# A nine-stage token tower: the filter spectrum computed in pieces inside earlier stages, expert weights gathered by GpSimd, and the token stage as one sequence

## What is computed

```python
h = _L0_tok_ref(x, L0_tok_emb, L0_tok_W, L0_tok_b)
h = h + _L0_attn_ref(_layernorm(h, axis=-1), ...)
...
h = h + _L3_attn_ref(_layernorm(h, axis=-1), L3_attn_h0, L3_attn_numerators, L3_attn_denumerator)
h = h + _L3_ffn_ref(_layernorm(h, axis=-1), ...)
```

```python
H_trunc = jnp.fft.rfft(b, n=Lx, axis=-1) / jnp.fft.rfft(a, n=Lx, axis=-1)
h_trunc = jnp.fft.irfft(H_trunc, n=Lx, axis=-1)
H = jnp.fft.rfft(h_trunc, n=2 * Lx, axis=-1)
H_tf = h0.astype(H_causal.dtype) + H_causal
Y = jnp.einsum('bli,ijl->blj', X, H_tf)
```

## Time and profile before

| | |
|---|---|
| median of 3 runs | 849.91 us (846.54 to 850.06) |
| the profiled execution's own time | 854.18 us |
| its span | 852.4 us |
| mean granted clock of TensorE, as a share of full speed | 0.822 |

### The profile page before, as it was taken

How to read it: one execution, slowest core, us unless ns; L and a number is a source line. 1 busy time by engine, 2 the same in 40 slices (tenths; PEclk the granted TensorE clock), 3 DMA queues, 4 the chain that set the end, 5 groups by cost and what they waited for, 6 DMA issues and landing times. The chain is left out here.

```text
span 852.4 us, 12948 instructions
## 1 busy us (share of the span) xinstructions
PE 630.7 (74%) x4476; PEld 418.0 (49%) x4476; DVE 519.1 (61%) x1402; ACT 331.4 (39%) x635; POOL 273.4 (32%) x233
## 2 busy tenths in 40 slices
PE   1489755774879378999759999777877652988774
PEld 1446644653767252322347878672322111984653
DVE  0105588653465747567657884428365898744797
ACT  1123201342545223544335553113432974831453
POOL 6431921414030101001157774322001698600420
PEclk9879768686999558989859996566898866999987
DMA  8652231100000010000000000040000000000011
GB/s 275 192 174 69 76 80 45 66 2 1 1 1 0 1 67 1 0 2 1 33 6 12 13 7 12 1 176 0 1 0 31 5 0 0 2 3 1 1 26 25
DMA packets 18781, 30.02 MB, mean 35 GB/s; under 512 B 6434, under 2 KB 15650, under 8 KB 18082
## 3 DMA queue, kind: packets, MB, share of 16 engines
q1 hardware_dynamic: 16162, 19.80, 7.6%
q0 software_dynamic: 2560, 9.44, 3.5%
HBM read 27.25 MB, written 1.05 MB: 33 GB/s over the span
## 5 line engine op out<-in xcount | busy, mean ns | idle before, releaser
L156 POOL TENSOR_TENSOR norm_rstd<-norm_var,minus_half 128x16 f32<-128x16 f32 x16 | 47.4, 2961 | 316.6 <-DVE norm_var L150 316.6
L1247 ACT ACTIVATE m_g<-PS,w_slot 128x512 f32<-128x512 f32 x96 | 60.7, 685 | 73.4 <-PE PS L1301 64.4
L1200 DVE TENSOR_TENSOR m_gw<-m_g,PS 128x512 f32<-128x512 f32 x96 | 61.3, 682 | 41.1 <-PE PS L1309 27.4
L1301 PE MATMUL PS<-m_xT,w_slot 64*128 64x512 f32 x192 | 70.2, 684 | 6.9 <-ACT m_g L1247 6.8
L1325 PE MATMUL PS<-m_gw,w_slot 128*64 128x512 f32 x192 | 57.2, 666 | 0.0
L252 PE MATMUL PS<-w_base,tok_windows 128*128 128x128 f32 x128 | 21.4, 342 | 29.1 <-DMA tok_windows<-in_emb,tok_ids 21.1
L232 POOL DMA_INDIRECT tok_windows<-in_emb,tok_ids x32 | 30.5, 953 | 22.1 <-PE PS L263 9.6
L1309 PE MATMUL PS<-m_gT,m_sel 48*128 48x512 bf16 x96 | 24.1, 418 | 17.8 <-DVE m_gw L1200 12.1
L2047 ACT COPY rat_xf<-PS 64x512 f32<-64x512 f32 x32 | 33.1, 1034 | 10.4 <-PE PS L2103 10.1
L138 DVE BATCH_NORM_STATS2 norm_halves<-H 128x6 f32<-128x64 f32 x256 | 33.8, 209 | 1.3 <-PEq L2637 1.2
L252 PEld LDWEIGHTS PS<-w_base,tok_windows 128*128 128x128 f32 x128 | 19.4, 180 | 30.7 <-issue 13.3
(11 more groups left out here) (341 smaller groups left out, 1669.0 us busy)
## 6 DMA issues: line engine op xcount, KB each, us to landing
rff_routed<-in_routed SPq DMA_DIRECT2D x64, 129.0 KB, 2.1
rat_hf<-in_rat_taps SPq DMA_DIRECT2D x1, 2048.0 KB, 8.2
w_slot<-in_w_rat SPq DMA_DIRECT2D x1, 1589.0 KB, 12.0
w_slot<-in_w_win SPq DMA_DIRECT2D x1, 1378.5 KB, 5.8
...
```

The lines of the kernel that those rows point to most:

```text
L156: nc.gpsimd.tensor_tensor(N.rstd[:], N.var[:], C.minus_half[:], ALU.pow).then_inc(S["norm_rstd"], 1)
L1200: nc.vector.tensor_tensor(gw[:, i % 2, half, :], g[:, i % 2, half, :], gate_bank[half], ALU.mult)\
L1247: nc.scalar.activation(g[:, i % 2, half, :], hid_bank[(n - 1) % 3], ACT.Gelu, bias=b1[:, s:s + 1])\
L1301: nc.tensor.matmul(hid_bank[n % 3], w1[lane(half), s, :], pair_of(xT, pair)[lane(half)], start=True, stop=True).then_inc(S["hid_ps"], 1)
```

## The change

**Filter.** A class `Filter` takes the place of `Coefficients`. Its taps and constants are loaded in the batch-norm stage. PE transforms steps 0 to 3 in that stage's tail and 4 to 7 at the head of m1. ACT copies both parts out (`move`) and squares the denominator (`square`: steps 0 and 1 in the batch-norm stage, 2 to 7 behind the gelus of m1's steps i = 2 to 7). POOL makes sums and products in m1 (`ratio`, five instructions a step: steps 0 to 2 ahead of `norm_rstd(1)`, 3 to 7 behind it). DVE takes 32 reciprocals of 128 x 128, one in each of m1's steps 16 to 31 and m2's steps 0 to 15. POOL multiplies by them in m2 (`scale`). The rational stage starts with a finished spectrum.

**Rational stage.** The token norms and transforms come first, three of the eight moves to `rat_xf` go from ACT to DVE, four forward transforms and the moves that follow stand among the responses, and three PSUM banks instead of four serve the responses.

**Token and linear stages.** The token stage goes chunk by chunk (`ladder`, spacing 22) instead of in two rounds of four, and takes in the block that loaded the first constants. Expert segments of chunks 0 to 3 are gathered by 32 indirect transfers that POOL issues, 16 behind the window gathers and 16 at the start of the linear stage; SP loads chunks 4 and 5 once the windows of chunk 5 have come, and 6 and 7 in the linear stage. `add_shared` has chunks 0 and 1 ahead of `norm_rstd(1)` and 2, 3 and 4 behind it.

**Transposes that nobody reads.** m1's 24 are gone, m2's 44 stay, and the window stage gets 16 and then 126 in its first part and 70 in its last.

The core of the diff:

```diff
+            C.load(sp, "base")
             C.experts.load_route(sp)
+            sp.wait_ge(gathered[1], 16 * G4)
             C.load(sp, "early")
             C.load(sp, "gate")
-            C.experts.load(sp, range(CHUNKS // 2))
+            sp.wait_ge(gathered[5], 16 * G4)
+            C.experts.load(sp, (4, 5))
...
+            C.experts.gather(pool, range(0, CHUNKS // 4))
+            pool.wait_ge(S["const"], 1)
...
+            ladder([(34, lambda c: turn_windows(c, 0)), (52, lambda c: turn_windows(c, 1)), (71, turn_tails),
+                    (82, convolve), (117, turn_y)], 22)
...
+            C.experts.gather(pool, range(CHUNKS // 4, CHUNKS // 2))
             pool.wait_ge(C.sem("early"), C.count("early"))
-            for c in range(CHUNKS // 2):
+            for c in range(2):
                 C.experts.add_shared(pool, nc.gpsimd.tensor_tensor, c)
                 C.experts.add_bias(nc, C, c)
             norm_rstd(nc, pool, S, C, N, 1)
-            for c in range(CHUNKS // 2, CHUNKS // 2 + 1):
+            for c in range(2, CHUNKS // 2 + 1):
...
+    def find_rows(self, v, C):
+
+        v.wait_ge(self.route_loaded, 16)
+        self.nc.vector.tensor_scalar(self.rows[:], self.route[:, 0:CHUNKS // 2 * SEGS], float(P), C["lane"], ALU.mult, ALU.add)\
+            .then_inc(self.rows_ready, 1)
+
+    def gather(self, pool, chunks):
+
+        pool.wait_ge(self.rows_ready, 1)
+        for c in chunks:
+            for j in range(SEGS):
+                at = c * SEGS + j
+                self.nc.gpsimd.indirect_dma_start(
+                    self.routed[:, c, j, :], None, self.dram["routed"],
+                    bass.IndirectOffsetOnAxis(ap=self.rows[:, at:at + 1], axis=0)).then_inc(self.loaded[c], 16)
...
+        y_banks = [PS[0][:, 1, 0:CW], PS[1][:, 0, 0:CW], PS[1][:, 1, 0:CW]]
+
+        @block.sync
+        def _(sp):
+            C.load(sp, "coef")
+            C.filter.load(sp)
...
+            def move_spectra(s):
+                for k in range(2):
+                    C.filter.move(act, s, k, [PS[2 + k][:]])
+
+            move_spectra(0)
+            move_spectra(1)
...
+            C.filter.square(act, 0)
+            move_spectra(2)
+            C.filter.square(act, 1)
+            move_spectra(3)
...
+                    for s in range(STEPS // 2, 3 * STEPS // 4) if it else range(STEPS // 2):
+                        C.filter.scale(pool, s)
+                else:
+                    for s in range(3, STEPS) if it else range(3):
+                        C.filter.ratio(pool, s, scratch[:])
...
+                    C.filter.invert(v, 2 * STEPS + i)
+                elif i >= n_round:
+                    C.filter.invert(v, i - n_round)
...
+                if again and i < 2:
+                    move_spectra(6 + i)
+                elif again and 2 <= i < 8:
+                    C.filter.square(act, i)
...
-            rouse(nc, C, y_bank[1], 24 if again else 44)
+            if not again:
+                rouse(nc, C, y_bank[1], 44)
...
+                spectra(4)
             for k in range(2):
                 turn_x(0, k)
+            if again:
+                spectra(5)
             logits(0)
             hidden(0)
             hidden(1)
+            if again:
+                spectra(6)
+            pe.wait_ge(S["identb"], 1)
             turn_parts(0)
+            if again:
+                spectra(7)
+                for k in range(2):
+                    pe.wait_ge(C.filter.moved[k], STEPS)
...
+                    rouse(nc, C, PS[3][:, 1, :], 16)
+                if n == 560:
+                    pe.wait_ge(S["h_new"], W + 1)
+                if n % 4 == 0:
+                    if 58 <= n < 228:
+                        rouse(nc, C, PS[3][:, 1, :], 5 if n < 115 else 3 if n < 172 else 1)
+                    if 560 <= n < 660:
+                        rouse(nc, C, PS[0][:, 1, :], 2 if n < 620 else 4)
...
+    def transform(self, pe, C, s, k, to):
+
+        if s == 0 and k == 0:
+            pe.wait_ge(C.sem("coef"), C.count("coef"))
+            pe.wait_ge(self.loaded, 16)
+        if s:
+            pe.wait_ge(self.moved[k], s)
+        for c in range(2):
+            rows = slice((2 * k + c) * QUAD, (2 * k + c + 1) * QUAD)
+            self.nc.tensor.matmul(to[c], C["rat_spectrum"][rows, :], self.taps[rows, s * STEP:(s + 1) * STEP],
+                                  start=True, stop=True).then_inc(self.made[k], 1)
+
+    def move(self, act, s, k, parts):
+        act.wait_ge(self.made[k], 2 * s + 2)
+        raw = self.raw[s][:, k]
+        n = 2 // len(parts)
+        for j, ps in enumerate(parts):
+            ins = self.nc.scalar.copy(raw[:, j * n:(j + 1) * n], ps)
+        ins.then_inc(self.moved[k], 1)
+
+    def square(self, act, s):
+        act.wait_ge(self.moved[1], s + 1)
+        self.nc.scalar.activation(self.of(s), self.raw[s][:, 1], ACT.Square).then_inc(self.squared, 1)
+
+    def ratio(self, pool, s, scratch):
+
+        pool.wait_ge(self.moved[0], s + 1)
+        pool.wait_ge(self.squared, s + 1)
+        of = self.of(s)
+        self.nc.gpsimd.tensor_tensor(self.inv[:, s], of[:, 0], of[:, 1], ALU.add).then_inc(self.power, 1)
+        num, den = self.raw[s][:, 0], self.raw[s][:, 1]
+        if s:
+            pool.wait_ge(self.sums, 2 * s)
+        self.nc.gpsimd.tensor_tensor(scratch, bcast(num[:, 1], 1, 2), den, ALU.mult).then_inc(self.terms, 1)
+        pool.wait_ge(self.terms, 2 * s + 1)
+        self.nc.gpsimd.tensor_tensor(den, bcast(num[:, 0], 1, 2), den, ALU.mult).then_inc(self.terms, 1)
+        pool.wait_ge(self.power, s + 1)
+        pool.wait_ge(self.terms, 2 * s + 2)
+        self.nc.gpsimd.tensor_tensor(of[:, 0], den[:, 0], scratch[:, 1], ALU.add).then_inc(self.sums, 1)
+        self.nc.gpsimd.tensor_tensor(of[:, 1], scratch[:, 0], den[:, 1], ALU.subtract).then_inc(self.sums, 1)
+
+    def invert(self, v, n):
+
+        s, k = n // 4, n % 4
+        at = self.inv[:, s, k * P:(k + 1) * P]
+        v.wait_ge(self.power, s + 1)
+        self.nc.vector.reciprocal(at, at).then_inc(self.inverted, 1)
+
+    def scale(self, pool, s):
+        pool.wait_ge(self.inverted, 4 * s + 4)
+        pool.wait_ge(self.sums, 2 * s + 2)
+        self.nc.gpsimd.tensor_tensor(self.of(s), self.of(s), bcast(self.inv[:, s], 1, 2), ALU.mult).then_inc(self.ready, 1)
...
-            for s in range(STEPS + 1):
-                if s < STEPS:
-                    square(s)
-                if s == 1:
-                    norm_rstd(nc, pool, S, C, N, 1)
-                if s:
-                    ratio(s - 1)
...
+            move_xf(0)
+            move_xf(2)
+            for g in range(PAIRS // 2):
+                if g in (2, 5, 6):
+                    move_xf({2: 4, 5: 6, 6: 7}[g])
+                real_parts(g)
...
+            pe.wait_ge(C.filter.ready, STEPS)
+            for g in range(PAIRS // 2):
+                respond(g)
+                if g in (1, 3, 4, 5):
+                    forward({1: 4, 3: 5, 4: 6, 5: 7}[g])
```

433 lines of the change are left out of this document (211 added, 222 removed).

## The result

The changed kernel takes 898.71 us (median; 897.86 to 899.55) against 849.98 us before: a ratio of 1.058, with an interval of 1.055 to 1.061. The forecast was 838 us. The profiled execution has a span of 897.5 us.

What follows compares the result with a forecast made beforehand. No engine was taken to bound the kernel: stages run one after the other with barriers. Terms -36 + 27 + 10 - 11 - 6 + 3 + 1 = -12 gave 842 us profiled, 838 us median; range 811 to 868.

Steps and rivals of the forecast that it cites:

- the slower rival: Linear stage and m1: POOL's reads hold DVE everywhere, +18 and +37, sum +9, median 859 us; chance 0.28.
- Rational stage, -36: Rational stage: the spectrum's eight steps leave it, so the last response's successor on PE comes 36 us earlier; bounds 30 to 40.
- Token stage, -11: Token stage: 48 gathers instead of 32 bound it; -15, or -4 if DVE's stall returns in full; milder half taken, -11.
- Linear stage, +10: Linear stage: gathers and additions delay POOL's norm, +5.4, plus one more hold of DVE, 4.2 us; bounds +5 to +18.
- m1, +27: First expert stage: four parts, for head, round 1's norm, DVE against POOL, and reciprocals; +27 us, between +11 and +37.
- Part (b): First expert stage: round 1's norm waits behind three ratios, the third waiting for ACT's square; +13 us, between +7 and +16.
- Part (c): First expert stage: DVE against POOL in the second gating and the norm; +3 us, between 0 and +7.
- (a): Head of the first expert stage: 24 transposes go, sixteen matmuls and ACT copies come; +7 us, between +3 and +9.
- (d): First expert stage: sixteen small reciprocals in steps where DVE had room; +4 us, between +1 and +5.
- m2, +1: Second expert stage: sixteen small reciprocals, with POOL's eight products beside steps in which it idles; +1 us, -2 to +4.
- Window stage, -6: Window stage: new transposes raise the clock in the tail, giving 7 us back and costing one; bounds -11 to +5.
- The rival that they do nothing: Window stage and m1: transposes fail to raise the clock, window +3, m1 +30, sum 0, median 850 us; chance 0.12.

Runs made afterwards that it cites:

- e8: The changed kernel, but SP loads all 64 expert segments and POOL gathers none, token stage still one sequence: ratio 1.036 to the kernel before, token stage 91.8 us.
- the memsets: The changed kernel with POOL's five operations of each first-expert-stage ratio replaced by memsets that read nothing: ratio 1.035 to the kernel before, m1 135.9 us.
- v2_again: Changed kernel with token and linear stages as before the change, ratios and reciprocals moved, m2's 44 transposes dropped; rerun: ratio 0.972 to the kernel before, token stage 68.8 us.

## Why the prediction was wrong

The time lies far outside the range (811 to 868), on the side that was given 0.30, and past the slower rival's 859.

- **Rational stage, -36**: right, and by its own steps. DVE was ready 20 us in, the responses' successor at 54.7.
- **Token stage, -11**: the step that failed most, by 27 us. "I take the milder half" rested on the segment loads no longer coming at that time. But the change puts 16 more gathers there, and the wait ("a releaser outside of the core's engines") goes with the indirect gathers: late signals of PE, 10.4 us of DVE's time before and 39.3 after. The bound of -4 assumed that the wait comes once, in full; that more gathers mean more of it was not in the range at all. The segments taken off POOL gave 19 us of compute back (`e8`). Where no signals are late the stage took 72, which is near the forecast's 73 by luck: the two rounds take 68.8 there (`v2_again`), so the change makes the stage no shorter on such a chip either.
- **Linear stage, +10**: right in when the norm ends (34 us in), though in this trace DVE's variance came last, 1.6 us behind POOL's list; wrong in "one more hold of 4.2 us". The three additions held DVE's eight operations for some 11 us, one after the other, where one had held them for 2.8 before. That is 8 us more, and with the norm 11 us later it makes 19 of the +19.5, past even the bound of +18 with three holds. `e8` finds the same two parts, 11 for the gathers and 8 to 10 for the order of the additions.
- **m1, +27**: mis-sized but inside its bounds, +33.4. Part (b), +13, came out at 26.3 - 11.2 = 15.1, and it is two costs over each other: 9 us of waiting, and the holds. Part (c), "+3, between 0 and +7", is where the rule was discounted: by the memsets, holds are worth 14.7 us in this stage. Without holds and wait 126.7 - 117.3 = 9.4 us are left for the head and the reciprocals, (a) and (d), which had 11.
- **m2, +1**: it measured +10. The reciprocals cost 5.4 us of it; another 4.6 is not explained.
- **Window stage, -6**: -1.2 against the kernel before. The transposes gave 151.2 - 143.8 = 7.4 us in the changed kernel's traces, and 10.7 and 11.3 within a group, so the mechanism was right and its size near. What the term left out is the 6.2 us by which the changed kernel's window stage is longer without them. The rival that they do nothing is out.

Two slips in the sum are too small to matter: 23 - 11 is 12 and not 13 in part (b), and the -1 of the first block's barrier is not in the -12.

The slower rival named the mechanism of the linear stage and m1, and nearly its price: +18 and +37, against 19.5 and 33.4. It was given 0.28, because "most of DVE's gate products read PSUM, and DVE has slack in most steps". That holds for the products, and not for gating and norm, on which everything else waits. But it reaches 859 only. Of the 36 us by which the trace lies above its sum of +9, 24 are the token stage's and 9 are m2's, and no rival had them. The Trainium skill's rule (SBUF — State Buffer, "Who interferes with whom") was cited as that rival; the trace and the memsets agree with it in every place looked at: POOL's reads hold DVE operations with two SBUF inputs, and POOL's writes alone do not.
